# Scatter half of the sorted rows early into regions that two experts share, and clear all of the regions after the attention

## Time and profile before

| | us |
|---|---|
| median of 3 runs | 587.76 (585.2 to 589.01) |
| the profiled execution, its own time | 592.25 |
| its span | 590.5 |
| busy: PE, DVE, ACT, POOL | 385.7, 410.8, 338.7, 270.9 |

### The profile page before, as it was taken

The page is one execution under the profiler, slowest core; times in us unless marked ns, Lnnn a source line. Parts: engine busy times, 40 slices in busy tenths (PEclk is TensorE's granted clock), DMA queues, the critical chain, the costliest instruction groups (busy, mean ns, idle before and its releaser), DMA issues.

```text
span 590.5 us, 8438 instructions
## 1 busy us (share of the span) xinstructions
PE 385.7 (65%) x2424; PEld 261.2 (44%) x2424; DVE 410.8 (70%) x904; ACT 338.7 (57%) x617; POOL 270.9 (46%) x394
## 2 busy tenths in 40 slices
PE   0967458788878877888767796800100079999970
PEld 0743136555444444554433335700000068888860
DVE  4895737799999999999999245577920005676671
ACT  0343134598898898888878356535100057777740
POOL 7453013244454454444401024653277405777774
PEclk9989656588899899888988799765555579999995
DMA  9460201345555555545540000000021274777700
GB/s 208 26 150 1 54 19 41 82 123 123 121 123 123 124 122 123 123 123 124 141 102 17 0 1 0 2 0 1 10 81 55 84 222 114 198 196 185 205 19 0
DMA packets 70665, 52.61 MB, mean 89 GB/s; under 512 B 17667, under 2 KB 62215, under 8 KB 70620
## 3 DMA queue, kind: packets, MB, share of 16 engines
q1 hardware_dynamic: 64502, 47.60, 33.5%
q0 software_dynamic: 2560, 4.27, 2.1%
q10 hardware_dynamic: 3558, 0.20, 0.4%
HBM read 36.02 MB, written 17.07 MB: 90 GB/s over the span
## 4 chain that ended last, share of the span: by engine, by line
DVE 38%; PE 30%; POOL 11%; issue 11%; ACT 4%; DMA 3%; ACTq 1%; SPq 1%; POOLq 0%; DVEq 0%
DVE mxs L1553 10%; DVE big L1653 9%; PE ps L1393 7%; PE ps L1404 6%; DVE big L1625 6%; POOL sorted_rows L720 5%; PE ps L1064 2%; DVE gb L1467 2%; PE ps L1209 1%; PE ps L1222 1%; PE ps L1315 1%; POOL arena L689 1%; DVE proj L1783 1%; PE ps L1235 1%; POOL late_s L677 1%
## 5 line engine op out<-in xcount | busy, mean ns | idle before, releaser
L1625 DVE SCALAR_TENSOR_TENSOR big<-big,ps 128x1024 f32<-128x1024 f32 x64 | 74.6, 1215 | 15.1 <-ACT big L840 15.1
L1653 DVE SCALAR_TENSOR_TENSOR big<-big,ps 128x1024 f32<-128x1024 f32 x64 | 76.2, 1213 | 5.7 <-PE ps L1222 5.5
L1553 DVE TENSOR_REDUCE mxs<-ps 128x4 f32<-128x1024 f32 x64 | 76.4, 1216 | 1.9 <-PE ps L1094 1.8
L844 ACT ACTIVATE big<-big 128x1024 f32<-128x1024 f32 x64 | 66.1, 1052 | 7.7 <-DVE big L1653 7.4
L1919 DVE TENSOR_SCALAR arena<-ps,x_all 128x128 f32<-128x128 f32 x48 | 14.6, 347 | 79.4 <-PE ps L1413 78.2
L1209 PE MATMUL ps<-proj 128*128 128x256 f16 x256 | 45.8, 313 | 34.0 <-DVE mxs L1553 22.2
L840 ACT ACTIVATE big<-ps 128x1024 f32<-128x1024 f32 x64 | 63.5, 1014 | 3.0 <-PE ps L1209 2.5
L741 POOL DMA_INDIRECT out_dram<-arena,fidx x48 | 48.9, 1020 | 18.5 <-issue 18.2
L985 ACT ACTIVATE x_all<-x_all 128x128 f32<-128x128 f32 x48 | 16.7, 397 | 63.3 <-DMA x_all<-sorted_rows 63.3
L651 POOL CAST mtok<-mxs 128x8 bf16<-128x8 f32 x32 | 6.0, 189 | 101.8 <-DVE mxs L1553 101.8
L1393 PE MATMUL ps<-arena,big 128*128 128x256 f32 x192 | 47.3, 391 | 4.2 <-ACT arena L990 4.2
(11 more groups left out here) (290 smaller groups left out, 901.2 us busy)
## 6 DMA issues: line engine op xcount, KB each, us to landing
big<-in_L_ffn_w_dram SPq DMA_DIRECT2D x48, 256.0 KB, 3.3
qk_parts<-proj SPq DMA_DIRECT2D x16, 384.0 KB, 2.9
arena<-qk_parts SPq DMA_DIRECT2D x32, 192.0 KB, 3.4
arena<-qk_parts SPq DMA_DIRECT2D x32, 128.0 KB, 4.0
sorted_rows<-zrow SPq DMA_DIRECT2D x16, 198.0 KB, 3.0
x_all<-sorted_rows SPq DMA_DIRECT2D x24, 132.0 KB, 2.2
proj<-u_parts SPq DMA_DIRECT2D x48, 64.0 KB
x_all<-in_L_attn_x_dram SPq DMA_DIRECT2D x4, 512.0 KB, 6.4
```

What stands on the lines that cost most here:

```text
L844: nc.scalar.activation(W[par1][:, n, :], W[par1][:, n, :], ACT.Exp).then_inc(p_ready, 1)
L1553: nc.vector.tensor_reduce(mxs[:, b1 % 2, :, 2 * n:2 * n + 2], src, AX_X, ALU.max, negate=True).then_inc(unit_free, 1)
L1625: nc.vector.scalar_tensor_tensor(W[par][:, n, :], W[par][:, n, :], 10.0, f, ALU.add, ALU.mult).then_inc(unit_free, 1)
L1653: nc.vector.scalar_tensor_tensor(W[par][:, n, :], W[par][:, n, :], 0.05, slot_of("log", b, n), ALU.mult, ALU.add).then_inc(unit_free, 1)
```

## The change

- **Regions.** The 8 experts form 4 pairs. Each pair shares a region of 17 blocks of 256 rows (`RB` = 17): the even expert fills it from the first row upward, the odd one from the last row downward. So the first row of every expert is known before any token is counted. `side` is +1 or -1, `row_from` the first row, `blk_from` the first block of an expert. The tensor has `NBLK` = 69 blocks, the last always zero. A row has 133 floats.
- **Tiles.** Each expert has one fixed tile, its first (tiles 0 to 7); 15 further tiles (`XS`) are given out by count. `NS` = 23 in place of 24, in 4 rounds of which the last has 5 tiles. The first six tiles have constant expert and block numbers.
- **Halves.** Choice, count, place and weight run for each half (`best`, `places`, `weight_in`, `weight_out`), and the second half's prefix sum goes on from the first (`seg_in`). One scan of 128 elements with a reset at each expert (`seg`) takes the place of eight scans.
- **Scatter.** POOL scatters four token tiles of the first half, does the last root, scatters the other twelve, then the sixteen of the second half. It waits for a half's places and weights only.
- **Clearing.** SP issues eight pieces after its last attention DMA: 69 x 256 rows of 133 floats, 9.40 MB. Then it waits for the end of the attention and issues the weights of tiles 0 to 5, waits for the scatters, and issues the six row loads back to back. Later tiles load two numbers (expert and block) in place of one.
- **Middle stage.** POOL no longer squares or adds: `square_t` moves to ACT with a sum in the instruction (four instructions a group), as does `square_x`; `sum_t`, `sum_x` and `scale_t` go; `add_shift` is on DVE for all groups, four instructions each, and does the scaling too. The shift by the mean moves into two further numbers of each row (C+3, C+4), used in the expert stage. POOL makes eight small constant tensors before its first root.

```diff
-    NS = NT * P // TS + NE
-    ROW = C + 4
+    XS = (NT * P - NE) // TS
+    NS = XS + NE
+    RB = NT * P // TS + 1
+    NBLK = RB * NE // 2 + 1
+    ROW = C + 5
...
-                zeros(b)
...
+            left = NBLK * RS
+            for i in range(ZP):
+                zeros(left * (i + 1) // ZP - left * i // ZP)
+            sp.wait_ge(h_done, NB + 1)
...
+            for j in range(DEPTH):
+                weights_in(j, slice(j, j + 1))
+            sp.wait_ge(scat, 16 * NT)
+            for j in range(DEPTH):
+                blk = RB * (j // 2) + (RB - 1) * (j % 2)
+                rows_in(j, slice(blk, blk + 1))
             sp.wait_ge(rsem["x"], 1)
...
-            pool.wait_ge(rsem["i"], 1)
-            pool.wait_ge(step["xr"], NH)
-            pool.wait_ge(step["ids"], 2)
-            pool.wait_ge(z_stored, 16 * NB)
-            for t in range(NT):
-                nc.gpsimd.indirect_dma_start(xs_d, bass.IndirectOffsetOnAxis(ap=sl_i[:, t:t + 1], axis=0),
-                                             srow[:, t, 0:ROW], None).then_inc(scat, 16)
+            root(T(6, 0), T(7, 0), step["vd"], step["rd"], 1)
+
+            def scatter(h, lo, hi):
+                pool.wait_ge(rsem["i"], h + 1)
+                pool.wait_ge(step["xr"], h + 1)
+                for t in range(h * TH + lo, h * TH + hi):
+                    nc.gpsimd.indirect_dma_start(xs_d, bass.IndirectOffsetOnAxis(ap=sl_i[:, t:t + 1], axis=0),
+                                                 srow[:, t, 0:ROW], None).then_inc(scat, 16)
+
+            pool.wait_ge(z_stored, 16 * ZP)
+            scatter(0, 0, GT)
+            root(T(6, 1), T(7, 1), step["vd"], step["rd"], 2)
+            scatter(0, GT, TH)
+            scatter(1, 0, TH)
...
+            def square_t(g):
+                act.wait_ge(step["t"], 2 * g + 2)
+                if g:
+                    act.wait_ge(step["tsq"], g)
                 for i in range(GT):
                     t = g * GT + i
+                    sq = nc.scalar.activation(ysq[0][:, i * P:(i + 1) * P], u_sb[:, t, :], ACT.Square, scale=C ** -0.5, accum_out=tl[:, 9, t:t + 1])
+                sq.then_inc(step["tsq"], 1)
...
             def add_shift(g):
-                dve.wait_ge(step["a1"], g + 1)
-                nc.vector.tensor_tensor(t_of(g), t_of(g), be2c_bc[:, :].unsqueeze(1).to_broadcast([P, GT, C]), ALU.add).then_inc(step["ab"], 1)
+                dve.wait_ge(step["rb"], g // GH + 1)
+                for i in range(GT):
+                    t = g * GT + i
+                    s1 = nc.vector.scalar_tensor_tensor(u_sb[:, t, :], u_sb[:, t, :], tl[:, 3, t:t + 1], be2c_bc[:, :], ALU.mult, ALU.add)
+                s1.then_inc(step["s1"], 1)
...
+            def places(h):
+                pick = rt[:, 2, h * TH:(h + 1) * TH, :]
+                at = rt[:, 3, h * TH:(h + 1) * TH, :]
+                dve.wait_ge(step["ids"], 11)
+                dve.wait_ge(rsem["p"], 2 * h + 2)
+                chain(nc.vector.tensor_tensor(flat(3, h).rearrange("p (e t) -> p e t", t=TH),
+                                              ps[:, 2 + h, 0:TH * NE].rearrange("p (t e) -> p e t", e=NE), seg_in[:, :, :], ALU.add))
+                chain(nc.vector.tensor_tensor_scan(flat(4, h), seg[:, :], flat(3, h), 0.0, ALU.mult, ALU.add))
...
+            def weight_in(h):
+                d = rt[:, 1, h * TH:(h + 1) * TH, :]
                 dve.wait_ge(step["rd"], h + 1)
+                nc.vector.tensor_tensor(d, d, T(7, h).unsqueeze(2).to_broadcast([P, TH, NE]), ALU.mult).then_inc(rsem["e"], 1)
...
```

More of the change, by code:

```diff
@@ L1798, in _, with weight_out @@
+            def weight_out(h):
+                dve.wait_ge(rsem["s"], h + 1)
+                chain(nc.vector.tensor_reduce(rs[:, 0, h * TH:(h + 1) * TH], rt[:, 1, h * TH:(h + 1) * TH, :], AX_X, ALU.add))
+                nc.vector.reciprocal(srow[:, h * TH:(h + 1) * TH, C], rs[:, 0, h * TH:(h + 1) * TH]).then_inc(step["xr"], 1)
             for g in range(GH + 2):
@@ L1817, in _ @@
             weigh(3)
-            sum_t(3)
             var_o(0)
+            gate_o(0)
             weigh(4)
-            gate_o(0)
-            sum_t(4)
+            add_shift(0)
             weigh(5)
-            sum_t(5)
+            add_shift(1)
+            weigh(6)
             logits(0)
             add_x(0)
-            weigh(6)
             add_x(1)
-            sum_t(6)
             var_z(1)
             weigh(7)
-            sum_t(7)
+            add_shift(2)
             add_x(2)
+            add_shift(3)
             add_x(3)
@@ L1836, in _ @@
             gate_o(1)
-            for g in range(GH):
-                sum_x(g)
+            best(0)
             var_x(0)
-            for g in range(GH, NG):
-                add_shift(g)
+            add_shift(4)
+            add_shift(5)
+            places(0)
             logits(1)
-            for g in range(GH, NG):
-                add_x(g)
-            std_rows(0)
-            def over_e(v):
-                return v.unsqueeze(2).to_broadcast([P, NT, NE])
-            lo = lx[:, 0, :, :]
@@ L1859, in _ @@
-            for g in range(GH, NG):
-                sum_x(g)
-            var_x(1)
-            dve.wait_ge(rsem["p"], 2)
-            chain(nc.vector.tensor_copy(rt[:, 3, :, :], ps[:, 1, 0:NT * NE].rearrange("p (t e) -> p t e", t=NT)))
-            for e in range(NE):
-                sc = nc.vector.tensor_tensor_scan(rt[:, 4, :, e], ones[:, 0:NT], rt[:, 3, :, e], 0.0, ALU.mult, ALU.add)
-            chain(sc)
-            cnt, til, end, beg = (rs[:, 2 + i, 0:NE] for i in range(4))
-            chain(nc.vector.tensor_scalar(cnt, rt[:, 4, NT - 1, :], 1.0 / TS, (TS - 1) / (2.0 * TS), ALU.mult, ALU.add))
@@ L1871, in _ @@
-            chain(nc.vector.tensor_scalar(til, cnt, MAGIC, None, ALU.add))
-            chain(nc.vector.tensor_scalar(til, til, -MAGIC, None, ALU.add))
+            weight_in(0)
+            add_x(4)
+            weight_out(0)
+            add_x(5)
+            add_shift(6)
+            add_x(6)
+            add_shift(7)
+            add_x(7)
+            best(1)
+            var_x(1)
+            places(1)
+            weight_in(1)
+            weight_out(1)
+            cnt, til, end, beg, at = (rs[:, 2 + i, 0:NE] for i in range(5))
```

271 lines of the change are left out of this document (150 added, 121 removed).

## The result

| | before | after |
|---|---|---|
| median of the runs, us | 588.38 (4 runs) | 565.33 (4 runs, 563.54 to 565.84) |
| the profiled execution: time, span | 592.25, 590.5 | 563.54, 561.5 |

The ratio is 0.961 (95% interval 0.956 to 0.966), a gain of 23 us; 563.0 was forecast. The two profiled executions lie 29.0 us apart in span. To split that, I count from a mark behind the attention: POOL's copy of the token numbers, its first countable work there (332.47 before, 329.16 after).

What follows compares the result with a forecast made beforehand. DVE was taken to bound the attention and middle stage, POOL the scatters, PE and POOL the experts; 17.8 (earlier scatters) + 3.1 (expert start-up) + 3.9 (one tile less) = 24.8 us off 587.76 gave 563.0, range 556 to 573.

## What to carry to other kernels

When a serial stage at the end of a queue (here 32 scatters at 1.27 us on GpSimd) waits for another engine, what counts is only how much of that engine's queue stands ahead of its first item, and whether its later items ever wait. List that queue by half, and move whatever the first item doesn't need behind it: here that, with POOL's roots moved to suit, gave another 6 us over the changed kernel with no instruction added. And a transfer's rate may be carried from one row of a profile to another case only at the same length of its runs and the same busy share: 528-byte rows didn't get faster than 213 GB/s when the engines were full, and rows of 532 bytes went at half the rate of rows of 544.

## What the runs showed of the hardware

- **Bytes per row and DMA rate.** Stores of short rows to HBM from SyncE's queue, with the DMA engines full by the profile (share 1.18 to 1.25): 147 GB/s at 532 bytes, 208 to 213 at 528, 286 to 303 at 544. The rows lie one behind the other, so the length also sets where each starts. The Trainium skill, page DMA: Bandwidth & Descriptors, section "How a descriptor splits into AXI transactions", has beats of 32 bytes and extra beats for descriptors that don't start aligned. The direction agrees; its counts for rows of this size (18 or 25 beats in its example of 576 bytes) don't give a factor of two, and length and start weren't varied apart here. The 528-byte rate comes from another kernel with smaller pieces.
- **SyncE is held up by slow transfers ahead in its queue.** Eight pieces of the same number of rows took 52 us to issue at 147 GB/s and 28 us at 286 to 303, and the first load of weights behind them 8.7 and 4.2 us. Whatever stands behind such transfers in the same queue is issued late.
- **The time of the attention stage varies by 5 us between executions** (mark at 327.3 to 332.2) with the same instructions on PE, DVE and ACT; stages are to be compared from a mark behind it.
